# A two-layer recurrent model on one core: later tree layers, earlier attention, and a state scan's last product dealt out evenly

## The reference, cut to what matters

```python
xn = _layernorm(x)                       # layer 0
x = x + (xn + attention(xn)) * silu(experts(xn))
xn = _layernorm(x)                       # layer 1
s = xn + alpha * scan_layer(xn)          # the scan: 512 channels x 16 states, 512 tokens
g = silu(trees(xn))                      # 8 trees of depth 7, 255 nodes each
out = x + s * g
# scan_layer, for every channel and state n:
#   h_t = exp(dt_t * A_n) * h_(t-1) + dt_t * x_t * B_t[n];  y_t = sum_n h_t * C_t[n]
```

## Time and profile before

| | |
|---|---|
| median of 3 runs | 2654.51 us (2651.61 to 2655.56) |
| the profiled execution | 2673.1 us |
| its span, first to last instruction | 2671.0 us |
| mean granted TensorE clock | 0.940 of full speed |
| scan begins, ends | 776 us, 2652 us |
| starts of batches 1 to 7 | 1016, 1268, 1523, 1771, 2030, 2288, 2506 us |

### The profile page before, as it was taken

One profiled execution on the slowest core, in us unless ns is written; L12 is line 12 of the kernel. 1 busy time (PEld: TensorE's weight loads), 2 busy tenths in 40 slices (PEclk: granted clock), 3 DMA queues, 4 the chain that ended last, 5 costly groups with the idle time before them and its releaser, 6 DMA issues.

```text
span 2671.0 us, 37912 instructions
## 1 busy us (share of the span) xinstructions
PE 2218.0 (83%) x13128; PEld 1411.8 (53%) x13128; DVE 1862.8 (70%) x2832; ACT 1762.4 (66%) x3266; POOL 1738.8 (65%) x1416
## 2 busy tenths in 40 slices
PE   6677879999688879898989898889889988888761
PEld 4444557776445546555655465456445644564441
DVE  5878544543246877687668767876778667789888
ACT  3556633446367876888588867796778677766862
POOL 1000254424767988788888789887977797656566
PEclk9888989999899999999989999999999999999895
DMA  4000258874566668654765486448534754477776
GB/s 157 25 21 5 84 157 230 236 214 91 93 121 131 123 118 184 135 113 97 182 128 112 86 200 121 97 95 187 118 86 91 179 122 90 93 166 162 181 171 152
DMA packets 280191, 344.22 MB, mean 129 GB/s; under 512 B 64063, under 2 KB 209664, under 8 KB 280000
## 3 DMA queue, kind: packets, MB, share of 16 engines
q0 software_dynamic: 84080, 175.67, 35.1%
q1 hardware_dynamic: 175248, 144.83, 19.0%
q10 hardware_dynamic: 20672, 21.30, 2.3%
HBM read 198.00 MB, written 26.80 MB: 84 GB/s over the span
## 4 chain that ended last, share of the span: by engine, by line
POOL 24%; PE 16%; issue 14%; ACT 9%; DVE 9%; DMA 2%; POOLq 0%; DVEq 0%; SPq 0%; ACTq 0%
POOL arena L1668 9%; POOL acc_sb L1646 6%; POOL arena L1674 4%; POOL arena L1684 4%; DVE bank L1543 3%; PE bank L1785 2%; PE bank L1790 2%; PE bank L1802 2%; PE bank L1840 2%; ACT PT L1025 2%; PE bank L1917 2%; PE bank L1948 1%; ACT Pr L1056 1%; ACT bank L1168 1%; PE bank L1746 1%
## 5 line engine op out<-in xcount | busy, mean ns | idle before, releaser
L1668 POOL TENSOR_TENSOR arena<-arena 128x512 f32<-128x512 f32 x512 | 877.3, 1791 | 18.2 <-DVE arena L1534 16.1
L1646 POOL DMA_INDIRECT acc_sb<-ybuf,slot_idx x256 | 423.1, 1653 | 128.3 <-DMA ybuf<-arena 64.3
L1259 DVE TENSOR_REDUCE negmax<-bank 128x1 f32<-128x512 f32 x512 | 328.2, 682 | 200.6 <-PE bank L1785 199.9
L1168 ACT ACTIVATE bank<-arena,A_sb 128x512 f32<-128x512 f32 x512 | 354.4, 697 | 163.3 <-DVE arena L1548 136.4
L1543 DVE TENSOR_TENSOR_SCAN bank<-bank,arena 128x512 f32<-128x512 f32 x320 | 389.9, 1218 | 82.9 <-ACT bank L1168 45.3
L1674 POOL TENSOR_TENSOR arena<-arena 128x512 f32<-128x512 f32 x192 | 298.7, 1556 | 207.8 <-DVE arena L1543 207.7
L1025 ACT COPY PT<-bank 128x512 f32<-128x512 f32 x512 | 298.1, 592 | 200.9 <-PE bank L1790 171.5
L1056 ACT ACTIVATE Pr<-bank,negmax 128x512 f32<-128x512 f32 x512 | 353.3, 701 | 103.1 <-DVE negmax L1259 102.8
L1790 PEld LDWEIGHTS bank<-ident,Pr 128*128 128x128 f32 x2048 | 234.6, 147 | 288.8 <-ACT Pr L1056 225.1
L1785 PE MATMUL bank<-Kp,Qp 64*128 64x512 f32 x1024 | 307.6, 666 | 87.2 <-ACT PT L1025 52.1
L1790 PE MATMUL bank<-ident,Pr 128*128 128x128 f32 x2048 | 312.0, 292 | 59.4 <-ACT Pr L1056 58.6
(11 more groups left out here) (216 smaller groups left out, 3676.7 us busy)
## 6 DMA issues: line engine op xcount, KB each, us to landing
arena<-arena POOLq DMA_DIRECT2D x255, 512.0 KB, 5.3
arena<-bc_dram SPq DMA_DIRECT2D x256, 256.0 KB, 3.9
ybuf<-arena ACTq DMA_DIRECT2D x64, 256.0 KB
arena<-in_w_gate SPq DMA_DIRECT2D x64, 128.0 KB
arena<-in_w_up SPq DMA_DIRECT2D x64, 128.0 KB
arena<-in_w_down SPq DMA_DIRECT2D x64, 128.0 KB
arena<-in_X SPq DMA_DIRECT2D x8, 512.0 KB, 6.8
s_sb<-in_X SPq DMA_DIRECT2D x8, 512.0 KB
```

The costliest lines, as they stand in the source:

```text
L1168: act.activation(bank[DECAY[g % 2]][:, :], dt_sb[:, size_slot(b, cb), :], ACT.Exp, scale=A_sb[:, cb, n:n + 1]).then_inc(ssm_decay, 1)
L1259: dve.tensor_reduce(negmax[:, m % RING_STAT:m % RING_STAT + 1], bank[m % RING_S_ATT][:, :], AX.X, ALU.max, negate=True).then_inc(att_max, 1)
L1646: pool.indirect_dma_start(acc_sb[:, i, :], None, ybuf, bass.IndirectOffsetOnAxis(ap=slot_idx[:, b * TILES + i, k:k + 1], axis=0), bounds_c ...
L1668: pool.tensor_tensor(st_sb[:, g % RING_S, :], u_sb[:, size_slot(b, cb), :], B_sb[:, load % RING_BC, :], ALU.mult).then_inc(ssm_input, 1)
```

## The change: what it does

The filler's order becomes attention 2, attention 3, tree 0, attention 4, tree 1, attention 5, tree 2, attention 6, attention 7, trees 3 to 7 (`LEAD` = 4). The trees no longer read `xn1` where it was made: each batch's `xn1` and `x1` and the scan layer's sum `fin_sb` are stored to DRAM and loaded again, `xn` into `g1` or a free half of `s_sb`, the other two into a free part of `AT`. The last product and sum leave `ssm_fin` (but for batch 7) and become `tree_gate`, two products and two sums of 128x512 on VectorE at the end of a tree layer, and SyncE stores the result after them. The rows that the attention reads are loaded and normalised by `prepare`, some parts ahead. The units of a step go from 3.5 to 3.2 in batch 0, from 3.9 to 3.45 until the last attention is emitted, and from 2.4 to 3.1 after that. `c_by_pool` takes 3 steps of 8 in every batch, 24 of 64; before it took 32 of 64 in batches 0 to 5 and none in 6 and 7. Both come to 192.

```diff
+LEAD = 4
-FILL_IN_FIRST = 3.5
+FILL_IN_FIRST = 3.2
-FILL_PER_STEP, FILL_PER_LAST = 3.9, 2.4
+FILL_PER_STEP, FILL_PER_LAST = 3.45, 3.1
-SILU_AT, HEAD_AT, LAST_AT, READY_AT = 20, 22, 60, 4
+SILU_AT, HEAD_AT, LAST_AT = 20, 22, 60
+READY_AFTER, INPUT_AT = 8, 16
...
+    order = [("attention", b) for b in range(LEAD - 1)]
+    for b in range(LEAD - 1, NB - 1):
+        order += [("attention", b), ("trees", b - LEAD + 1)]
+    order[-1:-1] = [("attention", NB - 1)]
+    order += [("trees", b) for b in range(NB - LEAD, NB)]
...
+    def prepare(a):
+        if a not in ahead_of:
+            if done["gated"] >= a - 1:
+                E.att_load(a)
+                ahead_of[a] = 0
+        elif ahead_of[a] < READY_AFTER + 2:
+            if ahead_of[a] >= READY_AFTER:
+                E.att_ready(a, ahead_of[a] - READY_AFTER)
+            ahead_of[a] += 1
...
         E.tree_g(b)
         yield 2.0
+        while not back[0]:
+            bring_back()
+            if not back[0]:
+                yield 0
+        if b < NB - 1:
+            E.tree_gate(b)
...
         if b >= 1:
-            fill_until("trees", b)
             yield from tail(b - 1)
...
                 fill_until("attention", b + 2)
-                fill_until("begun", b + 1)
                 gather_until(b + 2)
...
     def attended(b):
-        return min(b + 2, NB)
+        return b + LEAD if b + LEAD < NB - 1 else NB
...
     def c_by_pool(g):
-        return g % 2 == 0 and g // SCAN < NB - 2
+        return g % 8 in (0, 3, 6)
...
+            def ssm_in(self, b, cb):
+                if cb:
+                    return
+                w.wait_ge(x1_norm, 2 * (b + 1))
+                sp.dma_start(xn_dram[b].rearrange("(t p) d -> p t d", p=P), xn1[:, :, :]).then_inc(xn_out, 16)
+                if b < NB - 1:
+                    sp.dma_start(x1_dram[b].rearrange("(t p) d -> p t d", p=P), x1[:, b % 2]).then_inc(x1_out[b % 2], 16)
...
+            def tree_back(self, b):
+                w.wait_ge(att_postmm, TILES * attended(b))
+                w.wait_ge(tree_gate, 4 * b)
+                w.wait_ge(stored, 16 * b)
+                w.wait_ge(x1_out[b % 2], 16 * (b // 2 + 1))
+                w.wait_ge(fin_out, 16 * (b + 1))
+                sp.dma_start(back_x, x1_dram[b].rearrange("(t p) d -> p t d", p=P)).then_inc(back_in, 16)
+                sp.dma_start(back_fin, fin_dram[b].rearrange("(t p) d -> p t d", p=P)).then_inc(back_in, 16)
+            def tree_gate(self, b):
+                w.wait_ge(tree_gate, 4 * (b + 1))
+                sp.dma_start(out[b].rearrange("(t p) d -> p t d", p=P), back_fin).then_inc(stored, 16)
...
+            def tree_gate(self, b):
+                half = TILES // 2
+                w.wait_ge(back_in, 32 * (b + 1))
+                for j in range(2):
+                    own = slice(j * half, (j + 1) * half)
+                    w.wait_ge(tree_g1, 2 * b + j + 1)
+                    dve.tensor_tensor(whole(back_fin[:, own, :]), whole(back_fin[:, own, :]), whole(g1[:, own, :]), ALU.mult).then_inc(tree_gate, 1)
+                for j in range(2):
...
+                    dve.tensor_tensor(whole(back_fin[:, own, :]), whole(back_fin[:, own, :]), whole(back_x[:, own, :]), ALU.add).then_inc(tree_gate, 1)
...
+                if b < NB - 1:
+                    dve.scalar_tensor_tensor(fin_sb[:, i, :], o, alpha_sb[:, 0:1], fin_sb[:, i, :], ALU.mult, ALU.add).then_inc(ssm_fin, 1)
+                    return
```

More of the change, by code:

```diff
@@ L107, in tree_early, with tree_input, tree_back, tree_gate @@
     def tree_early(self, b): pass
+    def tree_input(self, b): pass
+    def tree_back(self, b): pass
+    def tree_gate(self, b): pass
     def tree_begin(self, b): pass
@@ L165, in attention @@
             yield 2.0
+        next_tree = dict(zip(order, order[1:]))[("attention", b)]
+        next_tree = next_tree[1] if next_tree[0] == "trees" else None
         for n in range(ATT_STEPS + LAG_RAN):
+            if n == INPUT_AT and next_tree is not None:
+                E.tree_input(next_tree)
+            if 2 <= b + 1 < LEAD or b + 1 == NB - 1:
+                prepare(b + 1)
             E.att_step(b, n)
             yield 2.0
-        if b >= 1:
-            E.tree_early(b - 1)
+        if next_tree is not None:
+            E.tree_early(next_tree)
         for i in range(TILES):
@@ L190, in experts, with prepared, bring_back, beside_tree @@
             yield 3.0
-    def trees(b):
+    order = [("attention", b) for b in range(LEAD - 1)]
[3 more added lines that the diff above has]
+    order += [("trees", b) for b in range(NB - LEAD, NB)]
+    ahead_of = {0: READY_AFTER + 2, 1: READY_AFTER + 2}
+    def prepare(a):
[7 more added lines that the diff above has]
+            ahead_of[a] += 1
+    def prepared(a):
+        while ahead_of.get(a, 0) < READY_AFTER + 2:
+            prepare(a)
+            if a not in ahead_of:
+                yield 0
+    def trees(b):
+        back = [b == NB - 1]
+        def bring_back():
+            if not back[0] and done["tailed"] > b:
+                E.tree_back(b)
+                back[0] = True
+        def beside_tree():
+            if b + LEAD < NB - 1:
+                prepare(b + LEAD)
+        while done["normed"] < b + 1:
+            yield 0
         E.tree_begin(b)
@@ L213, in trees @@
         yield 2.0
-    done = {"attention": 0, "begun": 0, "trees": 0, "normed": 0, "gated": 0, "gathered": 0, "sized": 0, "inputs": 0}
+        while not back[0]:
+            bring_back()
+            if not back[0]:
+                yield 0
+        if b < NB - 1:
+            E.tree_gate(b)
+    done = {"attention": 0, "trees": 0, "tailed": 0, "normed": 0, "gated": 0, "gathered": 0, "sized": 0, "inputs": 0}
     def filling():
@@ L221, in filling @@
                 E.att_ready(b, half)
-        for b in range(NB + 2):
-            if b < NB:
+        for kind, b in order:
+            if kind == "attention":
+                yield from prepared(b)
                 yield from attention(b)
[L225 to L235, removed]
+            else:
+                yield from trees(b)
+            done[kind] = b + 1
     filler, owed = filling(), [0.0]
@@ L249, in fill_until @@
         while done[what] < count:
-            owed[0] -= next(filler)
+            owed[0] -= next(filler, 0)
     def gathers():
@@ L370, in tail @@
         E.ssm_store(b)
+        done["tailed"] = b + 1
     def last_gates(b):
@@ L1958, in ssm_h @@
                 elif b:
-                    w.wait_ge(ssm_fin, 3 * TILES * (b - 1))
+                    w.wait_ge(ssm_fin, TILES * (b - 1))
                 else:
```

96 lines of the change are left out of this document (64 added, 32 removed).

## The result

The changed kernel takes 2622.75 us (median of 4 runs, 2619.14 to 2630.47) against 2655.03 (4 runs, 2651.61 to 2658.8) of the kernel before: 32 us less, a ratio of 0.9872 with a 95% interval from 0.985 to 0.9893. The forecast was 2597, so the gain is a little more than half of the 58 us worked out. The profiled execution took 2619.15 us; its scan begins at 757.5 us. It is left out of what follows: from the scan's first step to the end it is 1895 us before and 1860 after, -35, close to the -32 of the medians.

What follows compares the result with a forecast made beforehand. TensorE was taken to pace the early batches outside steps 22 to 60, GpSimd and mutual waits those steps, VectorE the end. -128 early, +65 late, +5 small: -58, scaled 2597 us; forecast range 2560 to 2635, with rivals 2530 to 2665.

Steps and rivals of the forecast that it cites:

- the open piece of tree 7: After the last scan step: some 35 filler units remain and lie open there.
- One sign of being wrong: The forecast is wrong if SyncE's waits delay B or C; booked at 0, 28 us without cover.
- TensorE paces, so time goes with units: Other 26 steps per batch: 97 to 86 us in batches 1 to 5 (-56), batch 0 89 to 81 (-8).
- Steps 22 to 60: Paced by GpSimd and engines' mutual waits: 145.5 us each, -58 over batches 1 to 5, -6 in batch 0.
- GpSimd's relief: Steps 22 to 60: GpSimd loses 4.75 of 19 products at 1.21 us, 5.7 us a batch.
- Floor 129: Steps 22 to 60: least time, GpSimd's busy 134.6 us less 5.7; ceiling 157.
- Batches 6, 7 and the end: Some 437 units at 0.98 us plus 20 for the closing: 448 us for 383, +65 (ends +43 and +96).
- Small terms: VectorE's last sums and gate operations, early C products, and the wait at `tree_gate`: +5 together; queue and added transfers 0.
- TensorE paces everything: Rival: early batches go by units throughout, -176, the end +43; -133, scaled 2522 us. Chance 0.2.
- The rule cited against this rival: Weight-load share measures TensorE, not busy time: a sixth spare in batches 0 to 5, so removing trees gives little there.
- Steps 22 to 60 don't shrink: Rival: mutual waits set those 38 steps; other steps give -64, end costs 65 to 96; 2676 us. Chance 0.13.
- The change cancels out: Rival: early gain -128 given back by end (+96), gates (15) and queue (28): +11 or no difference, 2654. Chance 0.07.

Runs made afterwards that it cites:

- the run of the order alone: The changed kernel (new order and units) with the old choice of who makes the products with C: 2637.5 against 2656.97 us for the kernel before, 0.9934.

## Why the prediction was half right

*Sign and place were right.* The early batches gain, the last two lose, the open piece of tree 7 is there. One sign of being wrong shows a little: GpSimd waited 9.2 us for B rows from SyncE's queue in batches 6 and 7, and 2.0 us in all before.

```profile
POOL arena L1785 <- DMA arena<-bc_dram: 9.2, 5, 4.1
```

Whether the store in that queue or the busier DMA engines (0.79 and 0.90) delayed them is open; with the store later it was 10.4 us. TensorE's clock, forecast at 1.0 in the late stretches, was 0.95 and 0.97 in batches 6 and 7. The sum of -58 became -35 as follows.

*The step that failed: "TensorE paces, so time goes with units", in the 26 steps of a batch outside 22 to 60.* It gave 86 us for each of batches 1 to 5 and 81 for batch 0, -64 together. Measured are 92.8 on average (463.8 in five batches for 485.7 before) and 103 for 89: -22 and +14, so -8. This is 56 us of error, more than the whole miss. The runs show two things in its place.

In batch 0 the units failed as a measure of time. Its first 22 steps held mostly a tree and now hold an attention, and TensorE's busy time rose from 65.0 us to 71.7 for fewer units. The run with trees at 3.2 units shows the kind's part directly, 65 us against 83 for equal units. The price of attention was in the prediction, 1.05 us a unit, and with it 87 us for batch 0's 26 steps, but 81 were booked. They took 103, since with so little filler the fixed part, some 15 us in 22 steps, weighs more.

In batches 1 to 5 the pacing failed. Beside the earlier trace rows, the three other stretches between batches before the change were:

```profile
1253.00:1349.00 96.00, 87.55 (x395) 59.10 (x394) 63.91 (x81) 66.36 (x99) 76.50 (x61) 0.98 0.71 165
1506.00:1597.00 91.00, 85.13 (x449) 58.21 (x447) 66.35 (x88) 65.04 (x110) 76.65 (x61) 1.00 0.72 160
1754.00:1853.00 99.00, 92.08 (x528) 60.94 (x527) 71.72 (x96) 71.58 (x129) 76.62 (x61) 0.98 0.64 148
```

In the five TensorE's busy time fell from 447 to 399 us, 48 where the forecast had 56. The time fell only from 484 to 461: the part without TensorE grew from 37 to 62 us, from 4 to 12 us a stretch to 11 to 17. It is 11 also in the two stretches that now hold most of a tree (85 and 92 us, with 265 and 317 matmuls). So taking filler out took TensorE's work out, and for half of it idle time came in its place. The kind of filler adds to it: the change takes three of the six trees out of batches 0 to 5, and more of what is left is attention. At attention's price alone, 26 x 3.45 x 1.05, the 26 steps come to 94 us, near the 92.8; but two of the five stretches are not attention, so the nearness is in part luck. What TensorE waits for in its idle time is argued, not shown: the waits above put ScalarE and VectorE (for scores) on the list, and no run changed that chain.

*Steps 22 to 60: right in batches 1 to 5, and too timid in batch 0.* 145.5 was forecast for each of 1 to 5, 144.9 is their mean (-62 for -58). That the mean came out so well is luck: the run of the order alone has 148.2 there, so order and units gave 45 us where 29 were booked, and GpSimd's relief 17 where 28 were. Batch 0 came down to 130 instead of 145 (-21 for -6), 135 of it without the new C share. Floor 129 was near as a number, but GpSimd's products alone don't set it: with 2.4 to 3.2 units and with any C share from three steps of 8 to none, batch 0's stretch stays at 130 to 135 us. With none it was:

```profile
845.00:979.00 134.00, 109.25 (x650) 68.22 (x648) 120.50 (x164) 93.83 (x191) 108.11 (x84) 0.93 0.71 145
```

GpSimd's busy time falls there from 124 of 131 us to 108 of 134, VectorE's rises from 108 to 120.5. So the limit may pass from the one to the other; what sets the floor is still open.

*GpSimd's relief.* 1.21 us a product gave 129 us busy in these stretches; the rows show 124 to 125, some 10 us less than before in place of 5.7, for a reason that is open. Over whole batches the price holds: each 48 products taken from GpSimd in the five lines above lower its busy time by 59 to 61 us, 1.2 to 1.3 us a product. In elapsed time it was half of what was booked: the C share brings 17 us in batches 0 to 5 where 6 x 5.7 = 34 were in the sum.

*Batches 6, 7 and the end.* 448 was forecast at 0.98 us a unit, 438.5 came: (438.5 - 20) / 437 = 0.96. The term was right in kind, and the run with 3.6 units a step agrees that there the amount of work counts. What the even C share brings there is nothing in the new order (438.5 for 440), and nothing by itself (GpSimd becomes the bound): the forecast's 17 us a batch given back to VectorE had no taker.

*Small terms.* Nothing of the +5 is to be seen. VectorE waited 10.8 us in 7 times for `g1` (15 booked at most), SyncE 69.5 us at the store, and moving both later gained nothing. The 28 gate instructions cost more than booked, 34 us of VectorE's time for 19 (next section).

*The rivals.* "TensorE paces everything" gave 2522 and fell with the 26 steps, where the part without TensorE grew. In the five stretches between batches its weight loads fell from 62% of the time to 55%, its busy share from 92 to 87%; the scan's first 25 us before the change had 65%. The rule cited against this rival (the Trainium skill, Perfetto Trace Analysis, Identifying the Most-Contended Engine), that weight loads tell TensorE's headroom better than its busy share, fits that: by them TensorE was nearly full in these stretches before and was not after. Its busy share tells the same here, so these stretches don't decide between the two measures. "Steps 22 to 60 don't shrink" fell with 157 to 145 us. "The change cancels out" came nearest in kind: 55 of 91 us are given back.

In sum: -91 for -128 (56 us too much in the 26 steps, 19 too little in the others), +55 for +65, 0 for +5.

## What to carry to other kernels

A unit of filler has no price of its own: it costs what its kind costs beside that step, and when a change re-orders the kinds, each stretch must be priced by the kind that will stand in it, not by the mixture that stood there. Thinner filler takes TensorE's work out, but idle time may come in its place: in the five stretches between batches 48 us of work less gave 23 us. Where three coupled engines are all busy some 80 to 87% and none 100%, try dealing out work between two that can trade it until their shares meet; in this one kernel that was worth some 20 us on top of the change. A budget that is met by due times has a cliff: 51 units too few in batch 0 made the kernel 66 us slower than the one before, by lumps in batches 5 and 6 and behind the scan.

## What the hardware showed beside it

Of the 28 gate instructions on VectorE (128x512, both inputs and the output in SBUF; min/median/max ns, first and last start) most take 0.68 us and a few up to 5.1:

```profile
L1608 DVE TENSOR_TENSOR AT<-AT,g x14: 677/692/3875, 1224.0 to 2536.9; 128x512 f32<-128x512 f32 x14
```

And the sums:

```profile
L1612 DVE TENSOR_TENSOR AT<-AT x14: 677/678/5099, 1225.3 to 2540.9; 128x512 f32<-128x512 f32 x14
```

The first four of them on VectorE's timeline (start, us):

```profile
1224.04 1.29 DVE L1608 TENSOR_TENSOR AT<-AT,g 128x512 f32<-128x512 f32 x2 [1.03 <-ACT g L1203]
1225.25 3.39 DVE L1612 TENSOR_TENSOR AT<-AT 128x512 f32<-128x512 f32 x2
```

GpSimd's timeline beside them:

```profile
1224.12 2.06 POOL L1763 DMA_INDIRECT acc_sb<-ybuf,slot_idx  x1 [0.16 <-issue]
1225.67 1.81 POOL L1785 TENSOR_TENSOR arena<-arena 128x512 f32<-128x512 f32 x1
```

The pair beside a GpSimd product takes 3.39 us, the pair without one 1.29. This holds for all 28: the eight that took over 0.7 us each overlap a tensor_tensor of GpSimd, and none of the other twenty does, with gathers (DMA_INDIRECT) beside some of them. The longest, 5.1 us, has two products beside it:

```profile
1792.74 5.70 DVE L1612 TENSOR_TENSOR AT<-AT 128x512 f32<-128x512 f32 x2
```

```profile
1793.21 1.86 POOL L1785 TENSOR_TENSOR arena<-arena 128x512 f32<-128x512 f32 x1
1794.41 1.56 POOL L1801 DMA_DIRECT2D arena<-arena  x1
1795.04 2.24 POOL L1785 TENSOR_TENSOR arena<-arena 128x512 f32<-128x512 f32 x1
```

In seven of the eight the VectorE instruction ends 0.55 to 0.56 us after the last product beside it; in the eighth a further product starts just as it ends. The Trainium skill (SBUF — State Buffer, 🔬 SBUF: two separate sides) says that a VectorE instruction with two SBUF inputs and a GpSimd instruction that reads SBUF exclude each other for the whole of the one that starts first. The trace agrees that VectorE's waits for the product's end. It doesn't show that the first to start goes first: the sum at 1225.25 is on record 0.42 us ahead of the product that it waits for.
